# Gated cross-attention and mixture of experts: seven half-size products for eight in five of eight slabs of the shared layer

## The chip, the cores and the metric

The kernel runs on one core of a Trainium2 chip. The metric is the device time of one execution in microseconds; of the kernel before three runs are given.

## What is computed

Thirty-two tiles x of 128 tokens and 512 features go through a gated cross-attention and then through a feed-forward part with eight routed experts (the best two for each token) and one shared layer, whose hidden width J is 1408:

```python
x = x + jnp.tanh(g_xattn[0]) * _L0_xattn_ref(_layernorm(x, axis=-1), ctx_512, L0_xattn_Wq, L0_xattn_w_kc_q, L0_xattn_w_kc_kv, L0_xattn_W_qr, L0_xattn_W_kr, L0_xattn_Wo)
x = x + jnp.tanh(g_ffn[0]) * _L0_ffn_ref(_layernorm(x, axis=-1), L0_ffn_router, L0_ffn_w_up_gate, L0_ffn_w_down, L0_ffn_shared_w_up_gate, L0_ffn_shared_w_down)
...
# in _L0_ffn_ref
routed = _moe_routed(x_flat, router, w_up_gate, w_down)
gu = jnp.einsum('td,dm->tm', x_flat, shared_w_up_gate)
gate, up = jnp.split(gu, [J], axis=-1)
shared = jnp.einsum('tm,md->td', jax.nn.silu(gate) * up, shared_w_down)
return (routed + shared).reshape(b, s, d)
```

## The kernel before

Each engine has an instruction stream of its own, written out by hand, and they are ordered by semaphores. Matmuls of full accuracy are made of three bf16 passes: every operand is held as an upper half (`HI`, a cast to bf16) and a lower half (`LO`, what the cast left, made by a subtraction), and `PASSES` is HI by HI, HI by LO, LO by HI. TensorE (`pe`) multiplies, ScalarE (`act`) makes upper halves and activations, VectorE (`dve`) and GpSimd (`pool`) make lower halves, SP (`sp`) issues loads, stores and transposing DMAs.

There are three parts. The **attention** runs over steps k up to 135. In it SP turns the normalised tile b for the router (`turn_xn2`, L426) once its lower part is ready and the logits matmul of the tile before (`lg_mm`) is done; TensorE multiplies it in `route` (L684). In the steps with k divisible by 4 SP also stores the tile's x1, which waits for VectorE's last operation on it.

The **shared layer** runs over steps v from 0 to 87. Step v handles slab g = v // 11 (512 tokens) and slice m = v % 11 (128 of the 1408 hidden features). TensorE makes in `gate_up(v)` (L729) 12 matmuls of 512 columns for the gate and 12 for up, four k tiles by three passes each, into one of two pairs of PSUM banks, and then in `down(v - 1)` (L746) 12 matmuls of 512 columns that add to four accumulator banks. ScalarE makes silu of the gate (`silu_step`, L975); VectorE multiplies by up, casts and subtracts (`hidden(v)`, L1218 to L1224), which gives the operand of `down(v)`. At the end of a slab VectorE adds the accumulators, scaled, to the output rows (`add_shared`, L1226, four tiles) and later the two expert rows of each token (`add_experts`, L1238), which GpSimd has gathered (`gather_rows`, L1547). The tokens of a slab lie transposed in `xs[g % 2]`; SP fetches the next slab's with four transposing DMAs when gate and up of the slab before are done.

Steps 0 to 21 (two slabs) run before the **experts**. At their start `choose` (L1266, VectorE) finds the two best experts of each token, TensorE ranks the tokens in step 4 (L783) and ScalarE copies the ranks (`rank_up`). The weights of the shared layer come in 22 pieces through a ring of three buffers (`load_wsh` on SP, `split_wsh` on ScalarE for the upper half, `lower_wsh` for the lower one); pieces 2m and 2m + 1 are slice m. The lower halves of pieces 0 to 11 are made by GpSimd in the attention's last steps, the other ten by VectorE in steps up to 5. Then 80 expert steps follow (`expert_step`, L805, matmuls of 352 and 512 columns), and steps 22 to 87 of the shared layer after them. In these SP, ScalarE, VectorE and GpSimd run steps 33 to 76 as a loop of two turns (`run_shared`, L332); TensorE's are written out.

## Time and profile before

| | us |
|---|---|
| median of three runs | 1926.85 (1925.59 to 1927.02) |
| the profiled execution | 1924.15 |
| its span, first to last instruction | 1922.4 |
| TensorE busy | 1874.0 (97%) |
| VectorE busy | 962.0 (50%) |
| ScalarE busy | 666.5 (35%) |
| GpSimd busy | 648.2 (34%) |
| mean granted clock of TensorE | 0.993 of full |

The span is what the profile covers; the run's time holds a little more at its ends. Busy time of TensorE counts each matmul's way through the array, and one matmul's end lies under the next one's start; the distance between starts, not the mean duration in a row, is what a matmul costs in a full stream.

### The profile page before, as it was taken

To read this page: it belongs to the slowest core of one execution; us is meant where nothing else is said; L and a number is where in the kernel's file an instruction comes from. 1 tells how busy PE (TensorE), PEld (TensorE's weight loads), DVE (VectorE), ACT (ScalarE), POOL (GpSimd) and SP (SyncE) were. 2 spreads that over 40 slices of the span, in tenths; PEclk is the share of its full clock that TensorE was granted. 3 is DMA by queue.
4 is the path that set the end of the run, shared out by engine and by line. 5 is a ranking of instruction groups with operands and counts; after the bars stand their busy time and mean duration, and the time that the engine had idled before them with its cause. 6 is when DMAs were issued, how large, how long until landed. Compare 5 with 4: busy or idle time off the path is not lost.

```text
span 1922.4 us, 32264 instructions
## 1 busy us (share of the span) xinstructions
PE 1874.0 (97%) x11972; PEld 1029.9 (54%) x11972; DVE 962.0 (50%) x1839; ACT 666.5 (35%) x1873; POOL 648.2 (34%) x683
## 2 busy tenths in 40 slices
PE   7799999999999998799999999999999999999999
PEld 7566666566666554344455555555544444444444
DVE  5777777777777775565422222222224323333244
ACT  4656666666566665210122222222110000000000
POOL 4644555554554665000233343344012101010101
PEclk9999999999999999899999999999999999999999
DMA  9446676666666666603299989899723512121202
GB/s 306 121 108 129 130 145 141 149 143 127 143 132 137 157 153 157 159 9 111 76 198 237 250 216 217 223 216 215 156 85 131 121 45 88 28 83 33 77 29 81
DMA packets 477332, 262.53 MB, mean 137 GB/s; under 512 B 410528, under 2 KB 416288, under 8 KB 477216
## 3 DMA queue, kind: packets, MB, share of 16 engines
q1 hardware_dynamic: 465696, 223.13, 50.5%
q0 software_dynamic: 11520, 37.76, 7.1%
q8 instruction: 85, 1.39, 0.3%
q14 instruction: 31, 0.25, 0.0%
HBM read 112.96 MB, written 48.23 MB: 84 GB/s over the span
## 4 chain that ended last, share of the span: by engine, by line
PE 87%; DVE 5%; ACT 3%; POOL 2%; DMA 1%; issue 1%; SPq 1%; DVEq 0%; ACTq 0%; POOLq 0%
PE o L610 14%; PE score L741 12%; PE o L832 8%; PE score L821 8%; PE p_bank L659 7%; PE p_bank L741 6%; PE m_bank L741 6%; PE o L753 6%; PE p_bank L821 4%; PE m_bank L821 4%; PE t_bank L753 3%; PE c_bank L753 3%; DVE arena L1033 2%; PE score L637 2%; PE c_bank L623 2%; PE t_bank L623 2%
## 5 line engine op out<-in xcount | busy, mean ns | idle before, releaser
L610 PE MATMUL o<-arena 128*128 128x512 bf16 x1536 | 354.0, 380 | 1.1 <-DVE arena L1033 1.1
L1033 DVE TENSOR_TENSOR arena<-arena 128x512 bf16<-128x512 f32 (+2 forms) x347 | 285.4, 828 | 20.7 <-ACT arena L931 4.9
L1423 POOL TENSOR_TENSOR arena<-arena 128x512 f32<-128x512 f32 x128 | 150.7, 1177 | 277.6 <-DVE arena L1054 275.6
L909 ACT ACTIVATE arena<-score,arena 128x128 f32<-128x128 f32 x512 | 181.9, 370 | 160.5 <-DVE arena L1125 160.5
L741 PE MATMUL score<-arena 128*128 128x512 bf16 x1056 | 235.3, 379 | 0.0
L610 PEld LDWEIGHTS o<-arena 128*128 128x128 bf16 x1536 | 148.0, 98 | 157.2 <-issue 1.7
L659 PE MATMUL p_bank<-arena 128*128 128x256 bf16 x1536 | 179.5, 274 | 0.7 <-DVE arena L1033 0.7
L741 PEld LDWEIGHTS score<-arena 128*128 128x128 bf16 x1056 | 103.3, 98 | 124.7 <-issue 0.2
L832 PE MATMUL o<-arena 128*128 128x512 bf16 (+1 forms) x720 | 168.4, 379 | 0.0
L1515 POOL TENSOR_TENSOR arena<-arena 128x1088 bf16<-128x1088 f32 x32 | 72.0, 2250 | 274.9 <-ACT arena L939 274.9
L659 PEld LDWEIGHTS p_bank<-arena 128*128 128x128 bf16 x1536 | 145.7, 98 | 24.1 <-DVE arena L1033 1.0
L821 PE MATMUL score<-arena 128*128 128x352 bf16 x960 | 151.5, 315 | 2.9 <-issue 2.9
L1016 ACT COPY arena<-o 128x512 f32<-128x512 f32 x80 | 46.9, 586 | 259.3 <-PE o L832 252.6
L753 PE MATMUL o<-arena 128*128 128x512 bf16 x528 | 129.1, 381 | 7.1 <-DVE arena L1033 7.1
L1033 DVE TENSOR_TENSOR arena<-p_bank,arena 128x512 bf16<-128x512 f32 x125 | 85.7, 686 | 93.8 <-ACT arena L926 93.8
L977 ACT ACTIVATE arena<-score 128x512 f32<-128x512 f32 x44 | 26.3, 597 | 302.1 <-PE score L741 294.9
L977 ACT ACTIVATE arena<-p_bank 128x512 f32<-128x512 f32 x44 | 26.3, 597 | 295.4 <-PE m_bank L741 288.2
L1220 DVE TENSOR_TENSOR arena<-arena,score 128x512 f32<-128x512 f32 x44 | 30.3, 688 | 195.4 <-ACT arena L977 189.5
L1220 DVE TENSOR_TENSOR arena<-arena,m_bank 128x512 f32<-128x512 f32 x44 | 30.3, 688 | 194.2 <-ACT arena L977 177.2
L821 PEld LDWEIGHTS score<-arena 128*128 128x128 bf16 x960 | 94.3, 98 | 58.9 <-issue 3.3
L741 PE MATMUL p_bank<-arena 128*128 128x512 bf16 x528 | 123.1, 384 | 1.0 <-issue 0.7
L741 PE MATMUL m_bank<-arena 128*128 128x512 bf16 x528 | 121.1, 379 | 0.0
(164 smaller groups left out, 2674.1 us busy)
## 6 DMA issues: line engine op xcount, KB each, us to landing
xrow_d<-arena SPq DMA_DIRECT2D x80, 256.0 KB
arena<-w_expert SPq DMA_DIRECT2D x32, 544.0 KB, 5.6
arena<-w_shared SPq DMA_DIRECT2D x22, 384.0 KB, 3.8
arena<-x SPq DMA_DIRECT2D x16, 512.0 KB, 4.9
arena<-x SPq DMA_DIRECT2D x32, 256.0 KB, 3.3
x_d<-arena SPq DMA_DIRECT2D x32, 256.0 KB, 2.6
xn_d<-arena SPq DMA_DIRECT2D x32, 256.0 KB, 2.5
arena<-x_d SPq DMA_DIRECT2D x8, 1024.0 KB
```

Source lines behind the costliest of these rows:

```text
L610: mm = pe.matmul(o_bank[b % 2][:, :], lhsT=cT[u % 2][:, a, h, :], rhs=M_w[:, w, head_of(hg, h), :], start=(hg == 0 and n == 0), stop=(hg = ...
L623: mm = pe.matmul(ctx_bank[u % 2][:, :], lhsT=kvN[g % 2][:, a, b % 2, :], rhs=pT[u % 4][:, w, :], start=(n == 0), stop=(n == 2))
L659: mm = pe.matmul(o, lhsT=B_w[:, a, t, cols], rhs=xT1[g % 2][:, w, t, :], start=(n == 0), stop=(n == 3 * KT - 1))
L741: mm = pe.matmul(dst[:, :], lhsT=wsh[m][:, a, col:col + P], rhs=xs[g % 2][:, w, t, :], start=(n == 0), stop=(n == 3 * KT - 1))
L753: mm = pe.matmul(acc_bank[t][:, :], lhsT=hsh[v % 2][:, a, t * P:(t + 1) * P], rhs=wsh[m][:, w, KT * 2 * P:], start=(m == 0 and n == 0), st ...
L821: mm = pe.matmul(banks[i % 2][:, 0:I], lhsT=xgT[i % 4][:, a, t, :], rhs=wx[e % 2][:, w, col:col + I], start=(n == 0), stop=(n == 3 * KT - 1))
L832: mm = pe.matmul(xd_bank[i % 2][:, :], lhsT=hxT[i % 4][0:IW[j], a, j, :], rhs=wx[e % 2][0:IW[j], w, col:col + D], start=(j == 0 and n == 0 ...
L909: mm = act.activation(prob[:, u % 4, h, :], score_bank[u % 2][:, h * S:(h + 1) * S], ACT.Exp, bias=neg_max[:, u % 4, h:h + 1], accum_out=d ...
L1033: return dve.tensor_tensor(dst, src, hi, ALU.subtract)
L1220: dve.tensor_tensor(h32[v % 2], silu[v % 2], up_bank[v % 2][:, :], ALU.mult).then_inc(h_mul, 1)
L1423: pool.tensor_tensor(prob[:, u % 4], prob[:, u % 4], rden[:, u % 4, :].unsqueeze(2).broadcast_to([P, 4, S]), ALU.mult).then_inc(normed, 1)
L1515: pool.tensor_tensor(wx[e % 2][:, LO, cols], wx_raw[:, n % 2, :], wx[e % 2][:, HI, cols], ALU.subtract).then_inc(wx_lo, 1)
```

## The change

From step 33 on (`SEVEN_FIRST`, slabs 3 to 7) gate and up of a step are computed as a product of 2 x 2 blocks by seven products. The blocks are: the contraction in two halves of two k tiles (j), the output features as gate or up (c), the 512 tokens as two halves of 256 (i). Each product is two k tiles by three passes, 6 matmuls with 256 columns, in a half of one of four PSUM banks that are taken in turn. Four of the seven need sums of token blocks (`combined`) or of weight blocks (`w_seven`). The weights' sums are made once for each of the 11 slices by GpSimd (`seven_sums`, `seven_lower`) and ScalarE (`seven_upper`) from weights that SP loads again (`load_raw`), in the last expert steps and in steps 23 to 31. The tokens' sums for slab g + 1 are made by VectorE in steps m = 4 to 9 of slab g (`x_combine`). The seven results are put together by one copy on ScalarE and seven additions of 256 columns on VectorE; silu then works in place on two halves in SBUF. `down(v - 1)` stands between the fifth and the sixth product. At m = 0 `add_shared` is cut in two. `run_shared` is written out on all engines.

Four edits lie in the attention's last steps and the first shared steps. `turn_xn2` of an odd tile comes ahead of the x1 store on SP. ScalarE's silu(1) comes after two more attention steps. `choose` comes after hidden(2), and the remaining weight pieces are split in steps 3 to 7 in place of before step 2 to step 5. The load of piece 14 is issued with those of 12 and 13.

```diff
@@ SP, attention step
+                if m == 0 and k // 8 - 2 < NG - 1:
+                    turn_xn2(2 * (k // 8 - 2) + 1, it)
                 if k % 4 == 0 and within(k // 4 - 1, NB):
                     b = k // 4 - 1
                     wait(sp, x1_done, b + 1, 4, it)
...
-                if m == 0 and k // 8 - 2 < NG - 1:
-                    turn_xn2(2 * (k // 8 - 2) + 1, it)
...
-            load_wsh(12)
-            load_wsh(13)
+            for n in range(12, 15):
+                load_wsh(n)
...
+            def load_raw(i):
+                wait(sp, w_summed, 4 * (i - 1), 0, None)
+                sp.dma_start(w_raw[i % 2].rearrange("p j t c n -> p (j t c n)"), w_shared[i, :, 0:KT * 2 * P])\
+                    .then_inc(w_raw_in[i % 2], 16)
...
+                if k in (71, 73, 75, 77, 79, 81):
+                    load_raw((k - 71) // 2)
...
+                if v in (24, 25, 26, 27, 29):
+                    load_raw(v - 18 if v < 28 else 10)
@@ TensorE
+                def product(r, xb, wb):
+                    for i in range(6):
+                        t, (a, w) = i // 3, PASSES[i % 3]
+                        mm = pe.matmul(seven_bank(n, r), lhsT=wb[:, a, t, :], rhs=xb[:, w, t, :], start=(i == 0),
+                                       stop=(i == 5))
+                    return mm
...
+                    pe.wait_ge(half_done, 7 * (n - 1) + U3)
...
+                product(0, x_block(0, 0), w_block(0, 0)).then_inc(product_mm, 1)
...
+                    pe.wait_ge(half_done, 7 * (n - 1) + U4)
+                product(1, x_block(0, 1), w_block(1, 0)).then_inc(product_mm, 1)
...
+                    pe.wait_ge(half_done, 7 * (n - 1) + GATE_B)
+                product(2, xc[:, :, 1], wc[:, :, 1]).then_inc(product_mm, 1)
...
+                    pe.wait_ge(half_done, 7 * (n - 1) + UP_A)
+                product(3, xc[:, :, 2], wc[:, :, 2]).then_inc(product_mm, 1)
+                pe.wait_ge(m1_up, n + 1)
+                product(4, xc[:, :, 0], wc[:, :, 0]).then_inc(product_mm, 1)
+                down(v - 1, None)
+                pe.wait_ge(half_done, 7 * n + GATE_A)
+                product(5, x_block(1, 1), wc[:, :, 3]).then_inc(product_mm, 1)
+                pe.wait_ge(half_done, 7 * n + U2)
+                product(6, xc[:, :, 3], w_block(1, 1)).then_inc(gu_mm, 1)
@@ ScalarE
-                if v < 6:
-                    split_wsh(10 + 2 * v)
-                    split_wsh(11 + 2 * v)
+                if 3 <= v < 8:
+                    split_wsh(6 + 2 * v)
+                    split_wsh(7 + 2 * v)
...
+            def seven_upper(i):
+                act.wait_ge(w_summed, 4 * (i + 1))
+                act.copy(w_seven[i][:, HI].rearrange("p n t k -> p (n t k)"),
+                         w_sums.rearrange("p n t k -> p (n t k)")).then_inc(seven_hi, 1)
...
+            def seven_step(v):
+                n = v - SEVEN_FIRST
+                act.wait_ge(product_mm, 6 * n + M1)
+                if n > 0:
+                    act.wait_ge(half_done, 7 * (n - 1) + U2)
+                act.copy(m1_sb, seven_bank(n, 0)).then_inc(m1_up, 1)
+                act.wait_ge(half_done, 7 * n + GATE_A)
+                act.activation(silu[v % 2][:, 0:HALF], silu[v % 2][:, 0:HALF], ACT.Silu)
+                act.wait_ge(half_done, 7 * n + GATE_B)
+                act.activation(silu[v % 2][:, HALF:], silu[v % 2][:, HALF:], ACT.Silu).then_inc(silu_done, 1)
...
+                if v in (23, 24, 25, 26, 27, 29, 30):
+                    seven_upper(v - 19 if v < 28 else v - 20)
@@ VectorE
-            choose()
-            lower_wsh(12)
-            lower_wsh(13)
             for v in range(2, 22):
                 hidden(v, None)
-                if v < 6:
-                    lower_wsh(10 + 2 * v)
-                    lower_wsh(11 + 2 * v)
+                if v == 2:
+                    choose()
+                if 3 <= v < 8:
+                    lower_wsh(6 + 2 * v)
+                    lower_wsh(7 + 2 * v)
...
+                dve.tensor_tensor(silu[v % 2][:, 0:HALF], m1_sb, seven_bank(n, 1), ALU.add).then_inc(half_done, 1)
...
+                dve.tensor_tensor(m16_sb, m1_sb, seven_bank(n, 2), ALU.add).then_inc(half_done, 1)
...
+                dve.tensor_tensor(m167_sb, m16_sb, seven_bank(n, 3), ALU.add).then_inc(half_done, 1)
...
+                dve.tensor_tensor(h32[v % 2][:, HALF:], m167_sb, seven_bank(n, 4), ALU.add).then_inc(half_done, 1)
+                dve.tensor_tensor(h32[v % 2][:, 0:HALF], m16_sb, seven_bank(n, 4), ALU.add).then_inc(half_done, 1)
+                if m == 0:
+                    add_shared(g - 1, None, (0, 1))
+                dve.wait_ge(product_mm, 6 * n + M4)
+                dve.tensor_tensor(silu[v % 2][:, HALF:], m167_sb, seven_bank(n, 5), ALU.add).then_inc(half_done, 1)
...
+                dve.tensor_tensor(h32[v % 2][:, 0:HALF], h32[v % 2][:, 0:HALF], seven_bank(n, 6), ALU.add)\
...
+                if m in (5, 8):
+                    link(dve.tensor_tensor(x_sums[:, 0], x32[:, 0, 1], x32[:, 1, 1], ALU.add))
+                    link(dve.tensor_tensor(x_sums[:, 1], x_sums[:, 0], x32[:, 0, 0], ALU.subtract))
+                    link(dve.tensor_tensor(x_sums[:, 2], x32[:, 0, 0], x32[:, 0, 1], ALU.subtract))
+                    link(dve.tensor_tensor(x_sums[:, 3], x32[:, 1, 0], x_sums[:, 1], ALU.subtract))
+                if m in (6, 9):
+                    link(dve.tensor_copy(combined[g % 2][:, HI, :, t, :], x_sums))
+                    lower(combined[g % 2][:, LO, :, t, :], x_sums, combined[g % 2][:, HI, :, t, :]).then_inc(x_summed, 1)
@@ GpSimd
+                if v in (23, 24, 25, 26, 27, 29, 30, 31):
+                    i = v - 20 if v < 28 else v - 21
+                    seven_lower(i)
+                    if i < JT - 1:
+                        seven_sums(i + 1)
```

## Rows read from the trace of the kernel before

**Rows 1.** page: busy us, share, instructions; shares of the chain that ended last

```profile
PE 1874.0 (97%) x11972; PEld 1029.9 (54%) x11972; DVE 962.0 (50%) x1839; ACT 666.5 (35%) x1873; POOL 648.2 (34%) x683
...
PE 87%; DVE 5%; ACT 3%; POOL 2%; DMA 1%; issue 1%; SPq 1%; DVEq 0%; ACTq 0%; POOLq 0%
```

**Rows 2.** windows: stretch, its us, busy us of each engine, clock, DMA

```profile
1750.00:1800.00 50.00, 50.00 (x234) 22.66 (x232) 20.98 (x33) 4.18 (x7) 8.31 (x12) 1.00 0.26 88
```

**Rows 3.** timeline of one step: start us, us, engine, line, operation

```profile
1423.53 1.46 PE L753 MATMUL o<-arena 128*128 128x512 bf16 x6
...
1426.12 2.75 PE L741 MATMUL p_bank<-arena 128*128 128x512 bf16 x12
...
1431.30 1.46 PE L753 MATMUL o<-arena 128*128 128x512 bf16 x6
1431.50 0.60 ACT L977 ACTIVATE arena<-p_bank 128x512 f32<-128x512 f32 x1 [6.26 <-PE m_bank L741]
1432.13 0.69 DVE L1220 TENSOR_TENSOR arena<-arena,m_bank 128x512 f32<-128x512 f32 x1 [3.53 <-ACT arena L977]
...
1432.85 0.43 DVE L1222 CAST arena<-arena 128x512 bf16<-128x512 f32 x1
```

**Rows 4.** timeline, attention: matmuls with 256 columns and what follows

```profile
710.78 2.79 PE L659 MATMUL p_bank<-arena 128*128 128x256 bf16 x24
...
713.41 2.75 PE L610 MATMUL o<-arena 128*128 128x512 bf16 x12
```

**Rows 5.** timeline, seam: idle time before an instruction in brackets

```profile
770.87 0.45 PE L684 MATMUL m_bank<-arena 128*128 128x24 bf16 x12
...
772.22 1.46 SPq L431 DMA_TRANSPOSE arena<-arena  x1
...
776.12 0.48 PE L684 MATMUL m_bank<-arena 128*128 128x24 bf16 x12 [4.80 <-DMA arena<-arena]
...
793.16 0.42 DVE L1271 TENSOR_REDUCE arena<-arena 128x32 f32<-128x256 f32 x1 [0.29 <-DVE arena L1119]
...
795.00 2.75 PE L741 MATMUL p_bank<-arena 128*128 128x512 bf16 x12
...
799.03 1.83 DVE L1033 TENSOR_TENSOR arena<-arena 128x768 bf16<-128x768 f32 x2
...
802.70 1.47 PE L753 MATMUL o<-arena 128*128 128x512 bf16 x6 [2.35 <-DVE arena L1033]
...
811.05 2.21 PE L753 MATMUL o<-arena 128*128 128x512 bf16 x6 [4.73 <-DVE arena L1033]
...
815.34 5.34 PE L741 MATMUL score<-arena 128*128 128x512 bf16 x24
```

**Rows 6.** groups by line and form: count, busy us, mean ns, idle before

```profile
L659 PEld LDWEIGHTS p_bank<-arena 128*128 128x128 bf16 x1536 | 145.7, 98 | 24.1 <-DVE arena L1033 1.0 <-issue 0.2
...
L1378 DVE TENSOR_TENSOR arena<-arena,score 128x352 f32<-128x352 f32 x40 | 20.9, 522 | 157.3 <-PE score L821 157.3
...
L1246 DVE SCALAR_TENSOR_TENSOR arena<-arena 128x512 f32<-128x512 f32 x64 | 47.9, 749 | 7.9 <-DMA arena<-xrow_d,arena 6.8
...
L1515 POOL TENSOR_TENSOR arena<-arena 128x1088 bf16<-128x1088 f32 x32 | 72.0, 2250 | 274.9 <-ACT arena L939 274.9
...
L1454 POOL TENSOR_TENSOR arena<-arena 128x256 f32<-128x256 f32 x16 | 11.6, 728 | 1.3
```

**Rows 7.** timeline, VectorE: one beside GpSimd's work, one with 2048 elements

```profile
785.59 1.27 DVE L1222 CAST arena<-arena 128x512 bf16<-128x512 f32 x1
...
859.41 2.29 DVE L1324 TENSOR_TENSOR arena<-arena 128x2048 f16<-128x2048 f32 x1
```

**Rows 8.** timeline after the experts: GpSimd's last gather, ScalarE's silu(24)

```profile
1422.18 0.94 POOL L1555 DMA_INDIRECT arena<-xrow_d,arena  x1 [0.30 <-issue]
...
1424.64 0.60 ACT L977 ACTIVATE arena<-score 128x512 f32<-128x512 f32 x1 [8.09 <-PE score L741]
```

**Rows 9.** timeline of the end: first matmuls of down(87)

```profile
1915.80 1.47 PE L753 MATMUL o<-arena 128*128 128x512 bf16 x6
```

More of the change, by code:

```diff
@@ L508, in _ @@
             sp.dma_start(y_sb, x1_t[0]).then_inc(y_in, 16)
-            for n in range(14, 2 * JT):
+            for n in range(15, 2 * JT):
                 load_wsh(n)
@@ L1570, in _ @@
                 pool.wait_ge(xo_out[i], 16 * NS // 4)
[L1571 removed]
+            run_shared(shared_step)
 def kernel(**inputs):
```

156 lines of the change are left out of this document (133 added, 23 removed).

## Prediction

> **What bounds the kernel now.** I read the page's busy table and its chain first, then the windows of the last 500 us, then the timeline of one step, then the few places where the tensor engine stands idle. TensorE is busy for 97% of the span and carries 87% of the chain [rows 1]. In the stage that the change rewrites it is at 100% in a 50 us window, at full granted clock, with VectorE busy for 21, ScalarE for 4 and GpSimd for 8 of the 50 us [rows 2], a window with much work for VectorE. So in that stage time is a number of matmul columns, and whatever takes columns away gives time back as long as the other engines keep up. One step there (one 128-wide slice of the hidden layer for 512 tokens) is 24 gate and up matmuls, as from 1426.12 to 1431.30, and 12 down matmuls, as from 1423.53 to 1426.12: 5.18 + 2.59 = 7.77 us, 0.2158 us each [rows 3].
>
> **Seven products for eight, on TensorE.** Steps 33 to 87, 55 of them. Removed are 24 matmuls of 512 columns, 24 x 0.2158 = 5.18 us [rows 3]. Added are 42 matmuls of 256 columns. The attention part has such matmuls, also with a new weight load for each: 24 of them take 710.78 to 713.41, 0.1096 us each [rows 4]. That group stands between waits, as each product will, and the next one starts without a gap. So 42 x 0.1096 = 4.60 us. Gain 0.576 us a step, 55 x 0.576 = 31.7 us; a product is 0.66 us and the new step 7.19 us. If each product boundary cost another 0.02 us, 7.7 us of it would go.
>
> A rule speaks against this: in the Trainium skill, "TensorE: Matmul & The Clock Gate", Back-to-back issue gap, a stream of weight loads and matmuls is said to sustain about 81 ns at 128 columns and 131 ns at 512. A line between these is 98 ns at 256: 24 x 0.131 = 3.1 us would become 42 x 0.098 = 4.1 us, a loss. The trace does not agree at 512 columns (215.8 ns), and the measured rows decide.
>
> **What VectorE takes over.** A step today is a multiply of 0.69, a cast of 0.43 and a subtraction, which I count like the multiply, with 0.03 us between them [rows 3], 1.9 us. Seven additions of 256 columns with a PSUM operand come to it. The form with 352 columns takes 0.522 us [rows 6], the one with 512 takes 0.69 [rows 3]: 1.04 ns a column, so 0.42 us at 256, and 7 x (0.42 + 0.03) = 3.2 us. (Bounds: 0.34, a straight half of 0.688, and 0.688 itself; I take 0.42, since the row with 352 columns lies nearest.) Beside them in each slab of 11 steps: four times two expert additions of 0.749 [rows 6] (6.2 us), four shared additions at about the same (2.9 us), and, new, the sums of the next slab's tokens. These are two additions over 1024 elements, eight links of 256 at 0.42 us, two casts and two subtractions over 1024. An operation of 2048 elements takes 2.29 us [rows 7], so 1.2 us for 1024, and a cast, 0.43 at 512, about 0.72: 2.5 + 3.6 + 4.0 = 10.1 us. Sum: 11 x 5.1 + 19.2 = 75 us for a slab of 11 x 7.19 = 79 us of TensorE. VectorE goes from under half busy to 95%, so its place in time must be looked at.
>
> Let a step start at 0 with product 0. Products 0 to 4 end at 0.66, 1.32, 1.97, 2.63, 3.29; down of the step before runs to 5.88; products 5 and 6 end at 6.54 and 7.19. A consumer sees a product 0.20 us after its end (silu at 1431.50 after 1431.30 [rows 3]). VectorE finishes the step before: last addition 0.2 to 0.65, product, cast, subtraction to 2.52; down needs that at 3.29: 0.77 us to spare. Then five additions to 4.8, and idle until product 5 at 6.74. Four banks are turned: product 0 of the next step needs the third addition (done 3.9, needed 7.19), product 1 the fifth (4.8, needed 7.85), product 2 the addition after product 5 (7.2, needed 8.5), product 3 the last one (7.65, needed 9.16). ScalarE's copy of product 0 is needed only by product 4, 2 us later. Extra work of up to 1.9 us fits into VectorE's idle time at no cost. Step m = 4 brings 2.75 us (expert additions and the first sum); then everything slides 0.8 us, the subtraction ends 3.2 us into the next step and down is just met. At m = 0 two shared additions stand ahead of product 5's addition and two behind the subtraction; the same 0.8 us slide, again just met. With 0.04 us for each handover in place of 0.03 the slides begin to show. I take 2 us of stalls in the 55 steps, bounds 0 and, with VectorE's operations 10% longer than counted (7.5 us a step against 7.19), 17 us.
>
> **The end.** Today down(86) covers the last silu chain; down(87) begins at 1915.80, by the step's 7.77 us 0.15 us late [rows 9]. Afterwards product 6 of step 87 comes behind down(86), and 0.2 + 0.45 + 0.72 + 0.46 + 0.72 = 2.55 us of VectorE lie open before down(87): plus 2.4 us. An idle of 2.35 us at 802.70 left the next six 512-column matmuls at full pace (1.47 us busy), one of 4.73 us at 811.05 did not (2.21 us) [rows 5], so I add no fall of the clock; it would be 1.7 us, since the 12 matmuls from 811.05 to 815.34 take 4.29 us and not 2.59.
>
> **The weights' sums.** For each of 11 slices GpSimd makes four sums of 256 elements (0.73 us in the nearest row, four 3.1 us) and a subtraction over 1024 (2.25 us at 1088) [rows 6], ScalarE a cast (at most 1.2 us, twice the 0.60 of half as many elements [rows 3]); SP makes eleven more loads of 512 KB. SP's loads wait for the sums of two slices before, with the experts' transposes queued behind; those sums are ready a step or two earlier, so that wait is empty. Between steps 73 and 82 of the experts they are hidden, for these engines have little to do there (GpSimd waited 275 us for ScalarE ahead of its expert weights [rows 6]). In steps 23 to 31 they stand in ScalarE's queue behind silu(v) and ahead of silu(v + 1). GpSimd's eight gathers end at 1423.1 [rows 8]; then a subtraction to 1425.4, sums to 1428.5, ScalarE's cast to 1429.6, and silu(24), today at 1424.6 [rows 8], comes at 1429.6. Its hidden row is ready at 1432.1 and down(24) wants it at 1431.3: 0.8 us of stall, up to 1.7 if GpSimd's work stretches VectorE's cast as at 785.59, where 0.43 became 1.27 us [rows 3, 7]. After that the ring of 3.1 + 1.1 + 2.2 = 6.4 us is shorter than a step of 7.77. I take 1.2 us, bounds 0 and 4. The loops that are written out add instructions to fetch; the tail of TensorE is written out today and shows no gap: nothing.
>
> **The seam between attention and shared part.** Idle before 776.12 is 4.80 us, before 802.70 2.35, before 811.05 4.73 [rows 5]. Three edits meet it. (1) SP's turn of the odd tile is put ahead of the x1 store. At 772.22 it comes after the store's wait for the last x1. Moved, it waits only for the logits matmul of 770.87 to 771.32 [rows 5], goes out at 771.45 and lands 0.75 us earlier: minus 0.75. The store goes 1.3 us later; nobody waits for it soon. (2) The choice of experts (793.16 to 799.03 on VectorE, 5.9 us) moves behind hidden(2), and ScalarE's two weight splits behind silu(3). silu(2) is then at 793.1, when the attention is over, hidden(2) done at 795.6, so the 2.35 us go. The choice ends at 801.5, hidden(3) at 803.4. TensorE: gate and up of step 3 from 795.00 [rows 5] to 800.2, down(2) to 802.8, ranks to 803.85, down(3) at once to 806.4. rank_up at 805.1 is in time. Step 4 starts at 806.4 and not at 815.34: minus 8.9 us, the slow-clock matmuls behind the second stall included. (3) One weight piece is loaded earlier and the later ones a step later: piece pair 12 and 13 is wanted at 821.9 and lowered at 805.4, pair 14 and 15 at 829.7 against 816.3, so nothing comes late. VectorE at steps 5 to 7 has 7.8 us for 7.77, with 2.5 us of slack: nothing. Together minus 9.65, bounds 6 and 11.
>
> **Sum.** 1922.4 - 31.7 + 2.0 + 2.4 + 1.2 - 9.65 = 1886.7 us of span. The median of the runs, 1926.85, is 4.45 us above the span of the profiled execution: 1891.1, I say 1891.
>
> **Rivals.** (A) VectorE becomes the bound: its operations or handovers are 5 to 10% longer than counted, it falls behind in m = 4 to 9 and down waits for the hidden row. For it: 95% busy. Against: each price is a row. 55 x 0.1 to 0.3 us = 6 to 17 us: 1895 to 1908. (B) The clock falls: stalls around m = 0 or at the ring of banks cost the full clock. A fall costs 1.7 us, as above [rows 5]. Once a slab it is 8.5 us, 1900; in each step it would be 93 us, 1984. Against: no forecast stall is over 1 us, and 2.35 us did no harm at 802.70. The Trainium skill has a rule for just this ("TensorE: Matmul & The Clock Gate", A second HAM failure mode: psum-queue depth-cycling): micro-idles from cycling through PSUM banks make the clock swing. Here the trace does not yet bear it out: the present stage turns over two pairs of banks at granted clock 1.00 [rows 2]. (C) Slower: a half-width PSUM addition costs what the full-width one does, 0.688 us. VectorE is then at 6.83 + 7 x 0.265 = 8.7 us a step and sets the pace: 55 x (8.7 - 7.77) = +50 us, with the seam and end 1971. It decides from 0.58 us an addition, where VectorE needs 7.89 us, the old step plus the seam's gain shared over 55. Against: 0.522 at 352 columns. (D) The change does not do what it says at the seam, because the weight pieces from HBM still release the chain: only 1 of 9.65 us comes, 1900. (E) Half-width matmuls do not come at half the price in this stage. A weight load lasts 0.098 us [rows 6] and is hidden under 0.110; with half of it open a matmul is 0.16 us, 42 of them 6.7 us, and 55 x 1.5 = 83 us make 1974. The gain is gone at 0.123. Against: the pace in the attention part [rows 4].
>
> **Chances.** Forecast (1886 to 1897) 0.62; A 0.17; B once a slab 0.07; D 0.08; C 0.02, B in each step 0.02, E 0.01; something of no size 0.01. The bound of "same" is 0.2%, 3.9 us, about what a measurement can tell here. Faster 0.94, same 0.01, slower 0.05. The range takes in the low end of the unknown costs (seam 11, no stalls, sum 1887, less 3 for the product pace) and A, most of B and D: 1884 to 1910.
>
> **What would show it.** In the profile after: silus or cast chains 7.2 us apart in steps 33 to 87, with 36 becoming 54 matmuls each; VectorE at 6.5 to 7 of 7.2 us; idle time of TensorE before the down matmuls naming VectorE's subtraction if A holds, granted clock under 1.00 if B does; additions of 0.42 us; step 4 of the shared part starting near 806; a gap of 2.6 us before the last 12 matmuls; a gap of about 1 us near 1431 less the seam's gain. The prediction is wrong if the distance of the steps is over 7.4 us or the seam keeps its two idles.

## The result, and the profile after

The changed kernel's median is 1902.41 us (four runs, 1901.93 to 1905.91), that of the kernel before beside it 1926.93: a ratio of 0.9878, 95% interval 0.9863 to 0.9894. The direction and the range held; the forecast of 1891 was 11.4 us too low. The profiled execution is the one of 1905.91 (span 1904.1). The same 24 matmuls of the attention begin at 96.94 us in it and at 94.36 in the profiled execution of the kernel before, so it was 2.6 us late near its start; I set that aside below.

Line numbers are new: L769 is `gate_up`, L786 the seven products, L832 `down`, L1059 silu, L1100 `seven_upper`, L1120 to L1124 ScalarE in a seven step, L1502 to L1524 VectorE in it, L1327 and L1329 multiply and cast of the old form, L1140 every lower half, L1353 `add_experts`, L1705 to L1712 the weights' sums, L1743 the gathers.

The page's busy rows and its chain (first line of it), to be held against [rows 1]:

```profile
span 1904.1 us, 35031 instructions
PE 1845.8 (97%) x12962; PEld 1128.1 (59%) x12962; DVE 1171.1 (62%) x2294; ACT 708.6 (37%) x1994; POOL 709.9 (37%) x730
PE 81%; DVE 6%; POOL 4%; ACT 3%; DMA 3%; issue 3%; SPq 1%; DVEq 0%; ACTq 0%; POOLq 0%
```

TensorE lost 28 us of busy time, but the span lost 18 only, and its share of the chain fell from 87 to 81%: the shares of GpSimd (2 to 4%) and of transfers (1 to 3%) grew. Where this happens is told by the windows (start and end; busy us and instructions of each engine, granted clock, DMA share, GB/s), of which the second answers to [rows 2]:

```profile
1450.00:1500.00 50.00, 43.57 (x211) 21.04 (x210) 34.31 (x46) 6.71 (x10) 32.48 (x34) 0.93 0.45 139
1750.00:1800.00 50.00, 50.00 (x378) 36.79 (x377) 42.68 (x86) 8.40 (x21) 8.21 (x10) 1.00 0.25 85
1850.00:1904.00 54.00, 48.36 (x344) 33.65 (x342) 39.57 (x79) 7.65 (x19) 7.91 (x10) 0.97 0.24 83
```

In the steady stage TensorE is full at clock 1.00, as before, and VectorE is at 85%. At 1450 to 1500, where GpSimd is busy for 32 of 50 us, TensorE misses 6.4 us and clock as well. One steady step in the timeline (start, us, engine, line), to be held against [rows 3]; the step goes from 1603 to 1610 us:

```profile
1602.85 1.46 PE L832 MATMUL o<-arena 128*128 128x512 bf16 x6
...
1605.44 0.82 PE L786 MATMUL score<-arena 128*128 128x256 bf16 x6
1606.09 0.82 PE L786 MATMUL p_bank<-arena 128*128 128x256 bf16 x6
1606.75 0.82 PE L786 MATMUL m_bank<-arena 128*128 128x256 bf16 x6
1607.40 1.47 PE L786 MATMUL score<-arena 128*128 128x256 bf16 x12
1608.71 0.82 PE L786 MATMUL p_bank<-arena 128*128 128x256 bf16 x6
1609.37 0.82 PE L786 MATMUL m_bank<-arena 128*128 128x256 bf16 x6
1610.02 0.81 PE L832 MATMUL o<-arena 128*128 128x512 bf16 x3
```

Six matmuls every 0.655 us, and 7.17 us from the one `down` to the next. ScalarE's 50 copies L1120 from 1535.85 to 1887.43 say the same of the whole stretch: 49 steps of 7.175 us on average, no stall among them.

The whole of TensorE's waiting from step 23 on is in the view of waits (waiter, releaser: us in total, times, longest):

```profile
PE o L832 <- DVE arena L1140: 11.4, 3, 6.4
PE score L786 <- DVE arena L1502: 4.2, 1, 4.2
```

They are four places, at 1427.12 (2.57), 1472.58 (6.43), 1517.66 (4.21) and at the end, 1896.34 (2.43). Behind three of them the clock fell; two are shown:

```profile
1472.58 2.74 PE L832 MATMUL o<-arena 128*128 128x512 bf16 x6 [6.43 <-DVE arena L1140]
1475.11 1.49 PE L832 MATMUL t_bank<-arena 128*128 128x512 bf16 x3
1476.39 1.30 PE L832 MATMUL c_bank<-arena 128*128 128x512 bf16 x3
...
1896.34 1.93 PE L832 MATMUL o<-arena 128*128 128x512 bf16 x6 [2.43 <-DVE arena L1140]
1898.06 1.48 PE L832 MATMUL t_bank<-arena 128*128 128x512 bf16 x3
```

Twelve matmuls from 1472.58 took 4.95 us in place of 2.59. Behind the third, 42 matmuls of 256 columns took 6.26 us in place of 4.59. The first three places together are 13.2 us of idle and, behind the second and the third, 2.4 and 1.7 us of clock: 17.2 us that the forecast had at 1.2. The first two stand where GpSimd makes the weights' sums; the third stands 34 us after the last of them.

**What stands ahead of each.** The first (ScalarE, GpSimd, VectorE, TensorE in the order of the chain):

```profile
1421.65 0.72 POOL L1708 TENSOR_TENSOR arena<-arena 128x256 f32<-128x256 f32 x1
1422.41 1.04 ACT L1100 CAST arena<-arena 128x1024 bf16<-128x1024 f32 x1 [12.76 <-POOL arena L1708]
1423.36 0.59 ACT L1059 ACTIVATE arena<-score 128x512 f32<-128x512 f32 x1
1423.99 0.69 DVE L1327 TENSOR_TENSOR arena<-arena,score 128x512 f32<-128x512 f32 x1 [12.20 <-ACT arena L1059]
1424.71 1.23 DVE L1329 CAST arena<-arena 128x512 bf16<-128x512 f32 x1
1425.97 1.09 DVE L1140 TENSOR_TENSOR arena<-arena 128x512 bf16<-128x512 f32 x1
```

ScalarE stands in its order behind a cast whose input GpSimd has not made; then cast and subtraction of the hidden row take 1.23 and 1.09 us. In the kernel before they take 0.43 [rows 3] and 0.69 (at 1441.08). The second:

```profile
1451.76 0.79 POOL L1708 TENSOR_TENSOR arena<-arena 128x256 f32<-128x256 f32 x1
1454.93 0.19 POOL L1739 COPY arena<-arena 128x8 f32<-128x8 f32 x1 [2.38 <-DVE arena L1353]
...
1464.69 0.94 POOL L1743 DMA_INDIRECT arena<-xrow_d,arena  x1 [0.30 <-issue]
1468.45 1.88 DVE L1353 SCALAR_TENSOR_TENSOR arena<-arena 128x512 f32<-128x512 f32 x2 [9.89 <-DMA arena<-xrow_d,arena]
1470.26 0.68 DVE L1327 TENSOR_TENSOR arena<-arena,m_bank 128x512 f32<-128x512 f32 x1
```

Eight gathers, 1.25 us each, can start only when VectorE has read the four tiles of the slab before; VectorE stands 9.89 us at `add_experts(4)`, and hidden(29) is queued behind it on the same engine. The kernel before has that wait too, and TensorE did not feel it:

```profile
1464.19 1.54 DVE L1246 SCALAR_TENSOR_TENSOR arena<-arena 128x512 f32<-128x512 f32 x2 [6.79 <-DMA arena<-xrow_d,arena]
```

The third is the same wait for slab 2, with the first addition of step 35 queued behind it, which the sixth product of that step waits for:

```profile
1515.74 1.54 DVE L1353 SCALAR_TENSOR_TENSOR arena<-arena 128x512 f32<-128x512 f32 x2 [5.79 <-DMA arena<-xrow_d,arena]
...
1517.66 0.86 PE L786 MATMUL score<-arena 128*128 128x256 bf16 x6 [4.21 <-DVE arena L1502]
```

The last gather goes out at 1499.98 and lands 15.7 us later, beside SP's four transposing DMAs, which took 18.14 us from 1492.81.

So three theories for the stalls: (a) ScalarE's in-order wait for GpSimd; (b) VectorE's cast and subtraction held up by GpSimd's work; (c) VectorE in its order behind the expert rows. And one more question, whether the step of 7.17 us is near VectorE's bound (rival A).

### The profile page after: what moved, and what is told of

The parts are those of the page before. It is cut to its first block, busy times and chain, and to the rows that moved or that the text cites. A ratio compares the mean times of both kernels' runs of the same rounds, so it can differ in the third digit from the quotient of the medians.

```text
span 1904.1 us, 35031 instructions
## 1 busy us (share of the span) xinstructions
PE 1845.8 (97%) x12962; PEld 1128.1 (59%) x12962; DVE 1171.1 (62%) x2294; ACT 708.6 (37%) x1994; POOL 709.9 (37%) x730
## 4 chain that ended last, share of the span: by engine, by line
PE 81%; DVE 6%; POOL 4%; ACT 3%; DMA 3%; issue 3%; SPq 1%; DVEq 0%; ACTq 0%; POOLq 0%
PE o L638 13%; PE o L911 8%; PE score L900 7%; PE p_bank L687 7%; PE score L786 6%; PE o L832 5%; PE p_bank L900 4%; PE m_bank L900 4%; PE score L769 3%; PE p_bank L786 3%; PE m_bank L786 3%; PE c_bank L832 3%; PE t_bank L832 3%; DVE arena L1140 2%; PE score L665 2%
## 5 line engine op out<-in xcount | busy, mean ns | idle before, releaser
L1140 DVE TENSOR_TENSOR arena<-arena 128x512 bf16<-128x512 f32 (+3 forms) x357 | 300.9, 849 | 17.0 <-ACT arena L1031 4.8
L786 PE MATMUL score<-arena 128*128 128x256 bf16 x1152 | 144.2, 273 | 4.2 <-DVE arena L1502 4.2
L1140 DVE TENSOR_TENSOR arena<-p_bank,arena 128x512 bf16<-128x512 f32 x125 | 85.7, 686 | 95.6 <-ACT arena L1008 95.6
L832 PE MATMUL o<-arena 128*128 128x512 bf16 x528 | 130.2, 383 | 11.4 <-DVE arena L1140 11.4
L900 PEld LDWEIGHTS score<-arena 128*128 128x128 bf16 x960 | 94.3, 98 | 58.8 <-issue 3.3
L786 PEld LDWEIGHTS score<-arena 128*128 128x128 bf16 x1152 | 112.9, 98 | 23.6 <-DVE arena L1502 4.7
L1484 DVE TENSOR_TENSOR arena<-arena,m_bank 128x352 f32<-128x352 f32 x40 | 20.8, 521 | 160.2 <-PE m_bank L900 160.2
L1484 DVE TENSOR_TENSOR arena<-arena,score 128x352 f32<-128x352 f32 x40 | 20.8, 521 | 159.3 <-PE score L900 159.3
L911 PEld LDWEIGHTS o<-arena 128*128 128x128 bf16 (+1 forms) x720 | 70.3, 98 | 77.1 <-DMA arena<-arena 2.4
L991 ACT ACTIVATION_READ_ACCUMULATOR arena<-score,arena 128x1 f32 x512 | 106.3, 208 | 0.0
L769 PE MATMUL score<-arena 128*128 128x512 bf16 x408 | 91.0, 380 | 0.0
```

What stands on the lines that cost most here:

```text
L769: mm = pe.matmul(dst[:, :], lhsT=wsh[m][:, a, col:col + P], rhs=xs[g % 2][:, w, t, :], start=(n == 0), stop=(n == 3 * KT - 1))
L786: mm = pe.matmul(seven_bank(n, r), lhsT=wb[:, a, t, :], rhs=xb[:, w, t, :], start=(i == 0), stop=(i == 5))
L832: mm = pe.matmul(acc_bank[t][:, :], lhsT=hsh[v % 2][:, a, t * P:(t + 1) * P], rhs=wsh[m][:, w, KT * 2 * P:], start=(m == 0 and n == 0), st ...
L900: mm = pe.matmul(banks[i % 2][:, 0:I], lhsT=xgT[i % 4][:, a, t, :], rhs=wx[e % 2][:, w, col:col + I], start=(n == 0), stop=(n == 3 * KT - 1))
L911: mm = pe.matmul(xd_bank[i % 2][:, :], lhsT=hxT[i % 4][0:IW[j], a, j, :], rhs=wx[e % 2][0:IW[j], w, col:col + D], start=(j == 0 and n == 0 ...
L991: mm = act.activation(prob[:, u % 4, h, :], score_bank[u % 2][:, h * S:(h + 1) * S], ACT.Exp, bias=neg_max[:, u % 4, h:h + 1], accum_out=d ...
```

## The experiments

Each number is a median; ratios are to the kernel before, run beside it on the same chip (medians 1924 to 1927 us), with the 95% interval.

**e1: the attention's edits alone.** The kernel before, with the turns ahead of the stores, silu(1) and the choice of experts later, the pieces as in the change; no seven products.

```diff
             for v in range(2, 22):
                 hidden(v, None)
+                if v == 2:
+                    choose()
```

> The kernel before with the four edits at the seam alone (turn of the odd tile ahead of the store, silu(1) later, choice of experts behind hidden(2), weight pieces split from step 3 on); no seven products. If the seam's gain is what the two traces show (fourth shared step at 806.25 in place of 815.34 us, 2.7 us won between the end of the attention's loop and 776 us), it is 1926.9 less 9 to 12, so 1915 to 1918 us. If that gain is lost again in the expert stage, which waits for its own loads, within 3 us of before. In the trace the two idles of 2.35 and 4.73 us before down(2) and down(3) are gone.

1914.15, 0.9936 (0.9923 to 0.9950): 12.2 us. **e2: the changed kernel without them**, the same lines taken back:

> The changed kernel without the four edits at the seam: seven products and all that they need. If the parts add up, it stands above the changed kernel (1902.4) by what the seam alone wins, so 1911 to 1914 us, and the stalls near steps 24, 28 and 36 stay as they are (2.6, 6.4, 4.2 us). If those stalls came from the seam edits they are gone, and it is at 1900 or less.

1914.90, 0.9939 (0.9926 to 0.9953): 11.4 us. 12.2 + 11.4 = 23.6, and both together gave 24.5, so the parts add. In e2 the three stalls stay (2.43, 4.71 and 4.08 us), so they do not come from the seam's edits. The seam brought more than the 9.65 of the sum, the seven products 11.4 where the other terms of the sum came to 26.1. The error is in the second part.

**e3: the weights' sums of slices 0 to 3 only**, used for all slices; the kernel leaves out those of slices 4 to 10. GpSimd's sums and ScalarE's casts in steps 23 to 31 are gone, of GpSimd's subtractions one is left in step 23, SP's seven loads for slices 4 to 10 are gone too, and the products are as many.

```diff
-                xc, wc = combined[g % 2], w_seven[m]
+                xc, wc = combined[g % 2], w_seven[m % 4]
...
-                if v in (23, 24, 25, 26, 27, 29, 30):
-                    seven_upper(v - 19 if v < 28 else v - 20)
```

> The changed kernel with the weights' sums of the first four slices only, used for all eleven (the output of slabs 3 to 7 is therefore not the reference's); loads, sums, cast and subtraction of slices 4 to 10 in steps 23 to 31 are left out. If these, standing in ScalarE's and GpSimd's queues and slowing VectorE, are behind the stalls: the idle before down(24) (2.6 us) and that before down(28) (6.4 us, and 2.4 us of slow clock behind it) go, and with them most of the 4.2 us at step 36: 1902.4 less 11 to 17, 1886 to 1891 us. If the cause is that four tiles' rows are gathered at one go behind the last addition of the group before, and VectorE's new work delays that addition: only the 2.6 us go and some of the delay, 1896 to 1900 us.

1888.43, 0.9811 (0.9797 to 0.9824). Of TensorE's waits from 1402 us on only the end's is left (the one of 0.7 us for "issue" is in every kernel here, the one before included):

```profile
PE o L830 <- DVE arena L1136: 2.4, 1, 2.4
PE p_bank L767 <- issue: 0.7, 1, 0.7
```

All three stalls come with the weights' sums, the late rows included: without the sums VectorE still waits 7.35 us for slab 1's rows, and TensorE does not notice. That the loads left out with them were not the cause is seen in e10 and e11 below, which have them all. This takes 14 us from the changed kernel (13 by the ratios), and the time is then near the forecast.

**e4: gathers tile by tile**, two a step, in place of eight at once.

```diff
+                if 25 <= v < 33:
+                    gather_tile(v - 21)
...
-                if v in (22, 28):
-                    gather_rows(0 if v == 22 else 1, None)
```

> The changed kernel with the expert rows gathered tile by tile (two gathers as soon as the tile four before is added, three steps ahead of use) in place of eight at one go. If late rows are the cause of the idles at steps 28 and 36, both go: 1902.4 less 6.4, 2.4, 4.2 and 2.0 us, 1886 to 1890 us, and VectorE waits for no expert rows; the 2.6 us at step 24 shrink too, as only two tiles' gathers stand ahead of the first sums. If the weights' sums are the cause, the stalls stay and it is 1900 us or more.

1898.47, 0.9858 (0.9843 to 0.9873): 4 us, between the two cases expected. VectorE's long wait for rows is gone, but at 1462.20 it now waits 5.69 us for `y_sb`, which is loaded only when all four tiles of slab 0 are stored, and idles of 1.2 to 5.0 us stay. Without the one at the end they are 11.6 us, against 13.2 in the changed kernel; the larger part of the gain is that the clock fell behind one of them only.

**e5: the last step of eight products**, so that `down(86)` stands behind gate and up of step 87.

```diff
+SEVEN_END = 87
...
-                if SEVEN_FIRST <= v < 88:
+                if SEVEN_FIRST <= v < SEVEN_END:
                     seven(v)
```

> The changed kernel, with its last step, gate_up(87), of eight products again: down(86) stands between gate_up(87) and down(87), and the step before it is still of seven. The view of TensorE's waits of the changed kernel has 2.43 us of idle ahead of down(87) at 1896.34, and the matmuls behind it ran 12 in about 4.45 us where 12 at full clock take 2.6. Theory 1 (the tail's loss is that VectorE's chain for the last step is longer in the form of seven products and has only down(86) beside it, and that the idle brings the low clock): the idle becomes that of the kernel before, nearly nothing; 0.58 us more of products, 2.4 less of idle, 1.2 to 1.9 less of low clock: 3 to 4 us less than the changed kernel, 1898.5 to 1899.5. Theory 2 (the low clock at the end comes in any case and the idle is only moved): at most 1 us less, 1901.5 to 1903.

1900.27, 0.9872 (0.9854 to 0.9889). The idle at the end is gone, and the low clock with it; the three stalls stay (2.54, 6.37 and 5.56 us):

```profile
1893.00 0.69 DVE L1146 TENSOR_TENSOR arena<-arena 128x512 bf16<-128x512 f32 x1
1893.75 1.47 PE L836 MATMUL o<-arena 128*128 128x512 bf16 x6
1895.05 0.81 PE L836 MATMUL t_bank<-arena 128*128 128x512 bf16 x3
1895.70 0.81 PE L836 MATMUL c_bank<-arena 128*128 128x512 bf16 x3
```

The median is 2 us lower than the changed kernel's. The ratio, against 0.9878, does not show it: the kernel before, run beside it, was lower as well (1924.15). Between theories 1 and 2 the trace says 1 and the times can't tell.

**e6: ScalarE's casts a step later**, gathers ahead of the sums, raw weights behind the stores.

```diff
-                if v in (23, 24, 25, 26, 27, 29, 30):
-                    seven_upper(v - 19 if v < 28 else v - 20)
+                if v in (24, 25, 26, 27, 29, 30, 31):
+                    seven_upper(v - 20 if v < 28 else v - 21)
```

> The changed kernel, with ScalarE's casts of the weights' sums (seven_upper) one step later each, so that the sum which a cast waits for is done before it; gathers of slabs 1 and 2 ahead of GpSimd's sums of their steps; and the raw weights' transfers behind the stores of the output on SyncE's queue. VectorE's work is as it was. The run with the weights' sums of slices 0 to 3 alone took all three stalls near steps 24 to 33 away and was at 1888.4, 14 us under the changed kernel. Theory a (the stalls are ScalarE's in-order wait of 12.76 us for GpSimd ahead of silu(24), and the rows that come late): the idles of 2.6, 6.4 and 4.2 us go, 1888 to 1892. Theory b (they are VectorE's casts, held up for as long as GpSimd's work beside them lasts, and with them add_experts): only the first goes, since the casts of steps 24 to 32 still stand beside GpSimd's sums; one or two idles of 4 to 6 us stay, 1895 to 1900.

1900.78, 0.9881 (0.9865 to 0.9898): no gain that the times can show, a little above what either theory gave. **e7: the cast of the hidden row on ScalarE** in steps 23 to 32 (the first two lines are in ScalarE's stream):

```diff
+                    act.wait_ge(h_mul, v + 1)
+                    act.copy(hsh[v % 2][:, HI, :], h32[v % 2]).then_inc(h_hi, 1)
...
-                wait(dve, h_mul, v + 1, 22, it)
-                dve.tensor_copy(hsh[v % 2][:, HI, :], h32[v % 2]).then_inc(h_hi, 1)
+                if not 23 <= v < SEVEN_FIRST:
+                    wait(dve, h_mul, v + 1, 22, it)
+                    dve.tensor_copy(hsh[v % 2][:, HI, :], h32[v % 2]).then_inc(h_hi, 1)
```

> The changed kernel, with the cast of the upper half of the hidden row in steps 23 to 32 made on ScalarE behind the silu and no longer on VectorE. The weights' sums and their order are as they were. In the changed kernel and in the one with gathers tile by tile that cast took 1.23 to 2.48 us beside GpSimd's sums where 0.43 is usual. Theory a (ScalarE's in-order wait for GpSimd and the late rows): ScalarE's queue has one operation more and its wait stays, the stalls stay, 1901 to 1906. Theory b (VectorE's casts are held up): VectorE gets 8 to 10 times 1 to 2 us back, the idle of 6.4 us at down(28) shrinks to under 3 and its low clock goes, 1893 to 1898.

1901.33, 0.9872 (0.9851 to 0.9893): as theory a said for it, with stalls of 1.75, 6.86 and 5.11 us. **e8: e5, e6 and e7 together:**

> The three edits together: the casts of the weights' sums a step later with the gathers ahead of GpSimd's sums, the cast of the hidden row in steps 23 to 32 on ScalarE, and the last step of eight products. If ScalarE's wait, VectorE's held casts and the tail are the whole of what the changed kernel loses: all idles from step 24 on are gone, 14 us for the three stalls and 3 to 4 for the tail, 1884 to 1887. If the rows of the expert sums come late for another reason (their transfers), one idle of 4 us stays near step 33 with its low clock, 1889 to 1892.

1896.49, 0.9853 (0.9834 to 0.9871), 4 us above even its second case. The first stall is gone in e6 and e8, and the later ones are there again in both: 3.23 us at 1462.22 and 2.75 at 1506.50 in e6, 3.66 and 5.91 in e8. The profiled execution of e6 was the fastest of its four (1894.51, 6 us under the median), so its trace may show less than the usual loss. VectorE in e6 (the idle in brackets):

```profile
1458.11 2.26 DVE L1353 SCALAR_TENSOR_TENSOR arena<-arena 128x512 f32<-128x512 f32 x2 [10.26 <-DMA arena<-xrow_d,arena]
1460.30 0.68 DVE L1327 TENSOR_TENSOR arena<-arena,m_bank 128x512 f32<-128x512 f32 x1
...
1504.57 1.54 DVE L1353 SCALAR_TENSOR_TENSOR arena<-arena 128x512 f32<-128x512 f32 x2 [4.32 <-DMA arena<-xrow_d,arena]
```

What was won ahead of the rows is lost in waiting for them. (My expectations of e3 and e7 name `down(28)` for the 6.4 us; counted in the timeline it is `down(29)`, which hidden(29) releases.) Removing a and b is not enough; c had not been met.

**e9: the rows alone**, tile by tile as in e4, and the expert sums of slab 0 in steps 23 to 26, so that `y_sb` is loaded a step sooner.

```diff
-                if 24 <= v < 32:
-                    add_experts(v - 24, None)
+                if 23 <= v < 32 and v != 27:
+                    add_experts(v - 23 if v < 27 else v - 24, None)
```

> The changed kernel with the way to the expert sums alone mended: the rows gathered tile by tile, two gathers a step, and the expert sums of slabs 0 and 1 in steps 23 to 26 and 28 to 31, so that the four rows of y that slab 1 starts from can be loaded a step sooner. ScalarE's casts and GpSimd's sums of the weights stand where the change put them, and so do VectorE's casts beside them, and the last step is of seven products. The kernel with gathers tile by tile alone was at 1898.5 with idles of TensorE of 2.3, 1.2, 2.0, 5.0, 1.2 and 2.4 us. Theory c (the larger part of the loss is that VectorE stands in its order at the expert sums, for rows or for y, with the hidden row of the next step behind it): the 5.0 and what follows it go, with the low clock, the first 2 to 3 us stay: 1890 to 1894. Theory a+b (ScalarE's in-order wait and VectorE's held casts are the larger part): under 3 us of gain, 1896 to 1899.

1894.92, 0.9850 (0.9832 to 0.9869): between the two forecasts, 1 us above theory c's and 1 us under the other's, so the times do not decide. The trace does, for c: the idle of 5 to 6 us before `down(29)` and the low clock behind it are gone. A rest of c stays: TensorE's longest idle is now 3.77 us at 1497.06, behind this wait of VectorE for the load of the rows that slab 2 starts from, and it happened to leave the clock full:

```profile
1495.18 1.41 DVE L1342 SCALAR_TENSOR_TENSOR arena<-o,arena 128x512 f32<-128x512 f32 x2 [5.41 <-DMA arena<-x_d]
```

The other idles, 1.53, 0.85, 0.85 and 1.66 us before `down(24)` to `down(27)`, are a pace. Steps 24 to 26 in e9:

```profile
1417.03 1.04 ACT L1100 CAST arena<-arena 128x1024 bf16<-128x1024 f32 x1 [10.48 <-POOL arena L1708]
1419.37 2.13 POOL L1712 TENSOR_TENSOR arena<-arena 128x1024 bf16<-128x1024 f32 x1
1419.33 2.48 DVE L1329 CAST arena<-arena 128x512 bf16<-128x512 f32 x1
...
1428.16 2.13 POOL L1712 TENSOR_TENSOR arena<-arena 128x1024 bf16<-128x1024 f32 x1
1428.10 2.49 DVE L1329 CAST arena<-arena 128x512 bf16<-128x512 f32 x1
...
1436.96 2.13 POOL L1712 TENSOR_TENSOR arena<-arena 128x1024 bf16<-128x1024 f32 x1
1436.89 2.49 DVE L1329 CAST arena<-arena 128x512 bf16<-128x512 f32 x1
```

GpSimd comes round every 8.79 us: a subtraction, four sums, two gathers of 1.25 us. TensorE's step is 7.77. So with one slice's sums and two gathers a step GpSimd is the bound of this stretch, through ScalarE's order and VectorE's cast. Since all four queues go round in one loop, the cast meets GpSimd's subtraction in every step and lasts as long as it.

**e10: e9, e5, and the sums spread** over steps 23 to 36, those of seven slices in fourteen steps; each is still there before its slice is wanted. ScalarE's cast comes a step behind the sum and SP's raw loads behind the stores, as in e6.

```diff
-                if v in (23, 24, 25, 26, 27, 29, 30, 31):
-                    i = v - 20 if v < 28 else v - 21
+                if v in (23, 25, 26, 28, 30, 32, 34, 36):
+                    i = {23: 3, 25: 4, 26: 5, 28: 6, 30: 7, 32: 8, 34: 9, 36: 10}[v]
```

It was run after **e11, the same with e7's cast on ScalarE**. Their expectations:

> All that was found, in one kernel: the expert sums as in the kernel with that alone; the eight remaining weights' sums spread over steps 23 to 36 in place of 23 to 31, each with ScalarE's cast a step behind the sum; the cast of the hidden row in steps 23 to 32 on ScalarE; the last step of eight products. If these are all the causes, TensorE has no idle over 1 us from step 23 on: 14 us less for the stalls and 2 to 3 less for the tail, 1884 to 1888. If GpSimd's sums in steps 34 and 36 hold VectorE up enough there, where it has 15% of its time free and not more, one or two idles of 1 to 3 us stand near 1500, 1888 to 1893.

> The best kernel so far (1884.6 us, no idle of TensorE left in the shared expert's part), with the cast of the hidden row in steps 23 to 32 on VectorE again as in the changed kernel; all else is that kernel's. Theory b (VectorE's casts held beside GpSimd's sums are a cause of their own): idles of 1 to 3 us come back near steps 24 to 32, with low clock behind the longer ones, 1887 to 1892. Rival (with the rows early and the sums spread, VectorE has the time for its held casts): no idle comes back, 1883 to 1887.

e11 1884.60, 0.9796 (0.9778 to 0.9813); e10 1885.29, 0.9793 (0.9777 to 0.9809). TensorE's waits from step 23 on, in e10:

```profile
PE o L836 <- DVE arena L1146: 2.7, 2, 1.7
PE p_bank L773 <- issue: 0.7, 1, 0.7
```

Both are 17 to 18 us under the changed kernel and 40 under the one before; by ratios 0.0085 or 16 us. The two can't be told apart, so the cast's engine makes no difference that can be measured once GpSimd is not the pace. In e10 VectorE's casts were still held up beside the sums (2.25 us at 1424.97, 1.87 at 1479.36) and no idle stood behind them: e10's rival held, theory b as a cause of its own is out. No run spreads the sums without moving ScalarE's casts, so how much of this is a is not told apart. The two idles that are left, 1.75 and 0.96 us in e10, are where I had feared them, beside GpSimd's work of steps 34 and 36:

```profile
1490.44 2.22 POOL L1720 TENSOR_TENSOR arena<-arena 128x1024 bf16<-128x1024 f32 x1 [5.88 <-ACT arena L1104]
1490.72 2.49 DVE L1146 TENSOR_TENSOR arena<-arena 128x512 bf16<-128x512 f32 x1
...
1493.27 1.47 PE L836 MATMUL o<-arena 128*128 128x512 bf16 x6 [1.75 <-DVE arena L1146]
```

**e12: three more additions of 256 columns on VectorE** behind the hidden row in steps 44 to 87; nobody reads them.

```diff
+MORE = 3
...
+                for i in range(MORE if v >= 44 else 0):
+                    dve.wait_ge(more_done, MORE * (v - 44) + i)
+                    dve.tensor_tensor(w_sums[:, 0].rearrange("p t k -> p (t k)"), h32[v % 2][:, 0:HALF], h32[v % 2][:, HALF:], ALU.add).then_inc(more_done, 1)
```

> The changed kernel with three more additions of 256 columns on VectorE behind the last operation of the hidden row in each of steps 44 to 87, each started behind the one before it; nobody reads them. It measures how far VectorE is from the bound in a step of seven products. VectorE is busy for 6.1 of a step's 7.17 us, and the additions are 3 times 0.46 us. If a step is the longer of TensorE's 7.17 and VectorE's sum: 6.1 + 1.4 = 7.5, so 0.3 more in 44 steps, 10 to 18 us over the changed kernel, 1912 to 1920, and TensorE idle in slices of it, in the steps with expert sums most. If VectorE's chain of waits adds to it in full (nothing of its idle can be used): 44 times 1.4, 1960 or so. If it has 1.4 us to spare at all steps: 1900 to 1904.

1920.63 (one run), 18 us over the changed kernel, just over the first case. A window of 200 us in it:

```profile
1650.00:1850.00 200.00, 189.69 (x1400) 134.18 (x1399) 184.01 (x398) 28.39 (x77) 16.45 (x20) 1.00 0.19 55
```

VectorE sets the pace here at 92% busy, not at 100 (TensorE is at 95%). Eleven steps take 85.2 us in place of 78.9, 0.57 a step more for 1.38 us of additions: 0.8 us was free in a step of the changed kernel on average, 11%. The steps are not alike: the four from `down(82)` to `down(86)` took 7.20 us each and paid next to nothing, the one from `down(59)` to `down(60)`, with expert sums in it, took 8.78.

## Why the prediction was right, and where it was not

The forecast of faster, for its two reasons, held. The median lies in the stated range (1884 to 1910) but above the band that the forecast itself was given (1886 to 1897, chance 0.62), where the range had been widened for rivals A, B and D, and none of the three happened as described. By its steps, measured against predicted:

- **Seven products**: 7.175 us against 7.19, 0.1092 us a matmul of 256 columns against 0.1096 [rows 4]. 55 steps, 427.35 us before, are 394.6: 32.7 us against 31.7. Rival E is out. (Its price was added up wrongly: the 83 us stand over the kernel before and not over the forecast, so it would have been near 2006 us and not 1974.)
- **VectorE's additions**: 0.41 to 0.42 us against 0.42 from the row with 352 columns [rows 6]; C is out. Two that do not wait for each other start 0.33 apart, so the engine was at 85% where I had summed 95%, and of the 2.0 us of stalls none came; A did not happen. It was not far away: in e12 1.4 us more a step cost 18 us.
- **The clock (B)**: it fell behind three idles that had another cause, and never in the ring of banks. From 1550 to 1850 the granted clock was 1.00, with TensorE busy for all of the 300 us. The Trainium skill's rule on micro-idles ("TensorE: Matmul & The Clock Gate", A second HAM failure mode: psum-queue depth-cycling), which the forecast had weighed, was not borne out by that trace.
- **The end**: 3.4 us against 2.4. The idle was 2.43 against 2.55. I took no fall of the clock, from one row of 2.35 us [rows 5]. The same 2.43 us left the clock up in e3, e4 and e9 and let it fall in e2, e6, e7 and the changed kernel, so this was a coin. It was worth 1.7 us over the 12 matmuls, of which 1.2 reached the end of the span (7.76 us from `down(87)` to the end, 6.52 in e9).
- **The seam**: 12.2 us (e1) against 9.65. Both idles of [rows 5] went, and `gate_up(4)` began at 806.25, predicted 806.4, and at 815.34 before; with the 2.6 us by which this execution was late from its start it is 11.7. The difference lies ahead of 776: idles of 0.57, 0.71 and 3.86 us where there were 1.81 and 4.80, and matmuls that had run at the low clock behind them now did not. I had 0.75 us for the moved turns, the price of the last one; the edit moves the turn of every odd tile. That this is where the rest came from is read off the idles, no run has it alone. D is out.
- **The weights' sums, +1.2 with bounds 0 and 4**: this is the term that failed, at 14 us by e3 and 17.2 by the trace. Its first part named the right chain. Silu(24) behind ScalarE's cast gave an idle of 2.57 us (0.8 to 1.7 predicted; VectorE's subtraction was held up as well as its cast). The step that failed is "After that the ring of 3.1 + 1.1 + 2.2 = 6.4 us is shorter than a step of 7.77". It was a sum over the sums' own ring alone, at undisturbed prices. That ring took 7.54 us (ScalarE's casts at 1422.41 and 1429.95), since the sums take 3.9 us when VectorE works beside them (1.05 for most in place of 0.73); it was still shorter than a step, and no idle came from it between 1429 and 1466. What broke the step was left out of it: the gathers of two slabs, 20 us, are on the same queue; and what is late on VectorE pushes the four tiles, the gathers wait for the tiles, VectorE waits for the gathers and the hidden row waits for VectorE. The kernel before bore a wait of 6.79 us in that place since VectorE was early there; I had not looked who was queued behind it.

Sum of the errors: -3.0 (products and stalls), +1.0 (end), -2.5 (seam), +16.0 (weights' sums), 11.5 in all, where 11.4 was measured. That the total held is in part luck: the seam and the stalls of VectorE were misjudged the other way by 4.5 us, and the error of the weights' sums alone would have given 1907 us, 3 under the edge of the range. The term itself, at 17.2 us, is four times its upper bound of 4.

What stays open: how the 14 us divide between c and GpSimd's pace. e9 took 5 to 7 us with most of c alone, some of it because the clock did not fall, e10 and e11 took 10 more with the pace and the end together (the end 1 to 3), and a without c took nothing. They are one loop through four queues, so no such division need exist. Nor did I separate the third stall's late transfers from the transposing DMAs beside them.

## What to carry to other kernels

Work that is put on an idle engine has to be summed with all that this queue does in the same steps, gathers and their waits included, at prices taken beside a busy VectorE, and compared with the step: in e9 8.79 against 7.77 us. Here the oversight cost about half of what seven products had gained. Where a stage turns out to be short of one engine for a few steps only, try to spread the work towards its deadlines (steps 23 to 36 in place of 23 to 31) before moving single operations: e10, which does so with the rows mended, gave 17 us, and e6 and e7 nothing that the times can show. And when an in-order engine waits harmlessly in the profile of before, name what stands behind that wait: it is the first to be late when the engine gets more to do.

## What the runs showed of the hardware

- A VectorE cast of 512 elements between SBUF operands took 0.43 us alone and 2.48 us beside a GpSimd subtraction of 2.13 us, both beginning within 0.07 us (e9, three times above); a VectorE subtraction took 0.69 alone, 1.09 beside sums of 256 and 2.49 beside that subtraction (e10). A forecast that stretches the cast only is short. The Trainium skill has this as a lock ("SBUF — State Buffer", Who interferes with whom): a cast in a mode that uses both of VectorE's port pairs, and an operation with two SBUF inputs, contend with GpSimd for the shared one, and the later one is blocked until the other's end. By that rule the trace agrees in length: 0.43 + 2.13 is 2.56, and 2.48 was measured. Which of the two came later is not shown: by the records it is the cast that begins first, by 0.04 to 0.07 us, and yet it is the one that is long; in e10 a subtraction began first (1424.78) and the cast behind it (1424.97) took 2.25.
- GpSimd pays too: its sum of 256 elements went from 0.72 to 1.05 us beside VectorE (changed kernel, 1420.05 and 1426.60).
- The granted clock after an idle of TensorE isn't a function of the idle's length alone: 2.43 us at the end left it full in three kernels and at half in four, 2.57 at 1427 and 3.77 (e9) left it full, 2.75 and 3.23 (e6) and 3.66 (e8) let it fall, and so did all from 4.08 (e2) on. This is 1 to 2.4 us an idle. That it is part of why executions of one kernel spread by 3 to 8 us here is likely and not shown; another part lies ahead of 97 us, where the same 24 matmuls begin between 92.29 (e11) and 96.94 (the changed kernel).
- Additions of 256 columns from PSUM that do not depend on each other start 0.33 us apart though each lasts 0.42; with a dependence it is 0.52, and 0.46 between SBUF operands (1480.41 to 1480.87). Sums of durations overstate an engine's load by that, and in e12 VectorE set the pace when it was shown 92% busy.
